# A perceiver layer: attention scores as twelve 32-row products in four row groups instead of four stacked 97-row ones

## The reference, cut to what matters

```python
q = (einsum('bqe,fe->bqf', layernorm(x), wq) + bq).reshape(1, 512, 16, 32)
k = (einsum('bke,fe->bkf', k_full, wk) + bk)      # k_full, v_full: the context twice over
scores = einsum('bqhd,bkhd->bhqk', q, k) / sqrt(32)
attn = softmax(scores, axis=-1)
ctx = einsum('bhqk,bkhd->bqhd', attn, v)
x = x + einsum('bqe,fe->bqf', ctx, out_proj_weight) + out_proj_bias
```

## Time and profile before

| | us |
|---|---|
| median of 3 runs | 1511.66 |
| lowest, highest | 1506.25, 1512.45 |
| span of the profiled execution | 1510.6 |
| PE busy (share of the span) | 1444.6 (96%) |
| DVE busy | 966.9 (64%) |
| ACT busy | 811.0 (54%) |
| 1024 score products (L612): busy | 311.5 |
| 2048 output products (L625): busy | 273.0 |

### The profile page before, as it was taken

The page is one execution under the profiler, slowest core; times in us unless marked ns, Lnnn a source line. Parts: engine busy times, 40 slices in busy tenths (PEclk is TensorE's granted clock), DMA queues, the critical chain, the costliest instruction groups (busy, mean ns, idle before and its releaser), DMA issues. The chain is left out here.

```text
span 1510.6 us, 21218 instructions
## 1 busy us (share of the span) xinstructions
PE 1444.6 (96%) x7952; PEld 910.1 (60%) x7952; DVE 966.9 (64%) x846; ACT 811.0 (54%) x865; POOL 25.9 (2%) x24
## 2 busy tenths in 40 slices
PE   6999999999799999999999999977799999999996
PEld 4888888888433333333333333325688878887884
DVE  7444444443588888888888888865355556555653
ACT  4122122121488888888888888832264445444551
POOL 2000000000300000000000000000000000000000
PEclk9999999999899999999999999998599999999999
DMA  6855455454685555555555555203044544454441
GB/s 199 253 174 207 176 187 201 167 201 161 189 213 115 112 111 111 111 115 118 116 117 116 112 111 111 56 5 110 28 140 156 178 166 164 153 183 163 163 147 57
DMA packets 136180, 214.26 MB, mean 142 GB/s; under 512 B 7624, under 2 KB 40520, under 8 KB 136144
## 3 DMA queue, kind: packets, MB, share of 16 engines
q1 hardware_dynamic: 136144, 213.78, 48.9%
HBM read 159.23 MB, written 51.38 MB: 139 GB/s over the span
## 5 line engine op out<-in xcount | busy, mean ns | idle before, releaser
L659 ACT ACTIVATE at_p<-at_s 128x1024 f32<-128x1024 f32 x512 | 496.8, 1023 | 91.2 <-PE at_s L612 91.0
L679 DVE TENSOR_TENSOR p_sum<-p_sum,at_p 128x2048 f32 (+1 forms) x208 | 476.8, 2292 | 58.4 <-ACT at_p L659 50.9
L612 PEld LDWEIGHTS at_s<-q_stack,at_k 97*128 97x128 f32 x1024 | 172.8, 189 | 249.0 <-ACT at_p L659 162.2
L612 PE MATMUL at_s<-q_stack,at_k 97*128 (+1 forms) x1024 | 311.5, 424 | 7.7 <-PEq L440 7.0
L625 PE MATMUL at_o<-at_p,at_v 128*32 128x512 f32 x2048 | 273.0, 605 | 0.1
L409 ACT ACTIVATE sc_k_hi<-sc_kp,sc_bk 128x512 fp32r<-128x512 f32 x64 | 44.2, 691 | 125.8 <-PE sc_kp L377 125.8
L139 ACT ACTIVATE sc_c_hi<-sc_c 128x2048 fp32r<-128x2048 f32 x16 | 30.7, 1918 | 150.6 <-PE sc_vp L384 137.6
L1267 DVE TENSOR_TENSOR ex_wi_lo<-ei_wi,ex_wi_hi 128x2048 fp32r<-128x2048 f32 x32 | 73.3, 2289 | 51.2 <-ACT ex_wi_hi L1226 51.2
L341 DVE SCALAR_TENSOR_TENSOR sc_k_lo<-sc_kp,sc_bk,sc_k_hi 128x512 fp32r<-128x512 f32 x64 | 48.0, 750 | 89.3 <-ACT sc_k_hi L409 89.2
L349 DVE TENSOR_TENSOR sc_v<-sc_vp,sc_bv 128x512 f32<-128x512 f32 x64 | 44.1, 690 | 88.8 <-PE sc_vp L384 88.8
L1244 ACT ACTIVATE ex_h<-ex_hp,ex_b_cur 128x256 f32<-128x256 f32 x128 | 53.7, 471 | 86.7 <-PE ex_hp L1125 86.2
(11 more groups left out here) (202 smaller groups left out, 1657.6 us busy)
## 6 DMA issues: line engine op xcount, KB each, us to landing
at_k<-k_hi_scratch SPq DMA_DIRECT2D x128, 256.0 KB, 4.7
ei_wi<-w_in SPq DMA_DIRECT2D x32, 1024.0 KB, 7.3
ei_wo<-w_out SPq DMA_DIRECT2D x32, 1024.0 KB, 5.3
sc_c<-ctx_t SPq DMA_DIRECT2D x16, 1024.0 KB, 8.0
k_hi_scratch<-sc_k_hi SPq DMA_DIRECT2D x16, 1024.0 KB, 4.0
k_lo_scratch<-sc_k_lo SPq DMA_DIRECT2D x16, 1024.0 KB, 6.1
at_k<-k_lo_scratch SPq DMA_DIRECT2D x64, 256.0 KB, 4.3
at_v<-v_scratch SPq DMA_DIRECT2D x64, 256.0 KB, 5.0
```

Source lines behind the costliest of these rows:

```text
L612: last = nc.tensor.matmul(s[r][:, a * NQ:(a + 1) * NQ], k[c][:, j, t * P:(t + 1) * P], q_stack[:, bass.ds(it // PER_GROUP * (HG * NQ) + j ...
L659: nc.scalar.activation(p[t % PR][:, pair * 2 * NQ:(pair + 1) * 2 * NQ], s[u % SR][:, :], ACT.Exp, scale=SCALE).then_inc(p_ready[t % PR], 1)
L679: nc.vector.tensor_tensor(sums, sums, p[t % PR][:, :], ALU.add).then_inc(p_summed[t % PR], 1)
```

## The change

The scores of a tile are no longer four products of 97 rows but twelve of 32 rows: for each of hi·hi, lo·hi, hi·lo, one for each head j, on partitions 32j to 32j+31 of keys and queries, accumulated in PSUM. The four heads of a part are on different row groups and write to different banks. Keys are loaded as they lie in scratch, [128, 512] hi and lo, three DMAs a chunk instead of four; there is no row of ones. This form has no shift row, so it is right only while scores are bounded. Therefore the old `attend` is kept as `attend_any`, in a block whose bodies stand in `If(flag < 1)` and which zeroes the accumulators and does the sum again (with two chunk buffers; `BY_PE = (3, 7)` of eight tiles). `find_maxima` moves from ahead of `attend` to behind it, with `attend_any` after it: `attend` runs always and unguarded, then come two guarded blocks.

PE's order changes too: a step is now all scores of tile t+1, then outputs of tile t-1. It waits for both buffers of the tile before its first product, and the two `s_ready` semaphores come in the last of the three parts. The middle iterations are a loop for each head group, so that `g` is a constant: nine iteration bodies instead of three.

```diff
-def load_keys(sp, a, c, g, chunk, k_hi_dram, k_lo_dram, v_dram):
+def load_chunk(sp, a, c, g, chunk, k_hi_dram, k_lo_dram, v_dram):
     keys, feats = bass.ds(chunk * CH, CH), bass.ds(g * P, P)
-    hi = k_hi_dram[feats, keys].rearrange("(j d) n -> d j n", d=D)
-    lo = k_lo_dram[feats, keys].rearrange("(j d) n -> d j n", d=D)
-    for part, src in enumerate((hi, lo, hi)):
-        sp.dma_start(a.k[c][part * D:(part + 1) * D, :, :].bitcast(F32), src).then_inc(a.loaded[c], 16)
+    sp.dma_start(a.k_hi[c][:, :].bitcast(F32), k_hi_dram[feats, keys]).then_inc(a.loaded[c], 16)
+    sp.dma_start(a.k_lo[c][:, :].bitcast(F32), k_lo_dram[feats, keys]).then_inc(a.loaded[c], 16)
     sp.dma_start(a.v[c][:, :, :], v_dram[keys, feats].rearrange("(t p) f -> p t f", p=P)).then_inc(a.loaded[c], 16)
...
-            def scores(it, u):
-                c, t, pair, r = u // 2 // KT, u // 2 % KT, u % 2, u % SR
-                if t == 0 and pair == 0:
+            def scores(it, g, t):
+                c = t // KT
+                if t % KT == 0:
                     pe.wait_ge(loaded[c], LOADS * (it + 1))
...
-                for a in range(2):
-                    j = 2 * pair + a
-                    last = nc.tensor.matmul(s[r][:, a * NQ:(a + 1) * NQ], k[c][:, j, t * P:(t + 1) * P],
-                                            q_stack[:, bass.ds(it // PER_GROUP * (HG * NQ) + j * NQ, NQ)],
-                                            start=True, stop=True)
-                last.then_inc(s_ready[r], 1)
+                for u in (2 * t, 2 * t + 1):
+                    if u >= SR:
+                        pe.wait_ge(p_ready[(u - SR) // 2 % PR], exped(it, u - SR))
+                    else:
+                        wait_reuse(pe, p_ready[s_last[u % SR] // 2 % PR], exped(it, s_last[u % SR]) - 2 * TPR)
+                for part, (keys, queries) in enumerate(((k_hi, q_hi), (k_lo, q_hi), (k_hi, q_lo))):
+                    for j in range(HG):
+                        rows, r = slice(j * D, (j + 1) * D), (2 * t + j // 2) % SR
+                        last = nc.tensor.matmul(s[r][:, j % 2 * NQ:(j % 2 + 1) * NQ], keys[c][rows, t % KT * P:(t % KT + 1) * P],
+                                                queries[rows, g, :],
+                                                start=(part == 0), stop=(part == 2))
+                        if part == 2 and j % 2 == 1:
+                            last.then_inc(s_ready[r], 1)
...
-            def iteration(it, last):
+            def iteration(it, g, ends_group):
                 for t in range(TILES):
-                    for u in (2 * t + AHEAD, 2 * t + AHEAD + 1):
-                        if u < 2 * TILES:
-                            scores(it, u)
-                        elif not last:
-                            scores(it + 1, u - 2 * TILES)
-                    outputs(it, t)
+                    if t + 1 < TILES:
+                        scores(it, g, t + 1)
+                    elif not ends_group:
+                        scores(it + 1, g, 0)
+                    elif g + 1 < NG:
+                        scores(it + 1, g + 1, 0)
+                    if t > 0:
+                        outputs(it, t - 1)
+                    elif not (isinstance(it, int) and it == 0):
+                        outputs(it - 1, TILES - 1)
...
+            scores(0, 0, 0)
+            for g in range(NG):
+                if g == 0:
+                    iteration(0, 0, False)
+                with pe.Fori(1 if g == 0 else 0, PER_GROUP - 1) as i:
+                    iteration(i + g * PER_GROUP, g, False)
+                iteration((g + 1) * PER_GROUP - 1, g, True)
+            outputs(ITERS - 1, TILES - 1)
...
-            with ExitStack() as s:
-                find_maxima(nc, s, k_hi_dram, k_lo_dram, ident, q_stack, bounded)
...
             with ExitStack() as s:
-                attend(nc, s, k_hi_dram, k_lo_dram, v_dram, q_stack, o_acc, p_sum, total_acc, a, late, late_dram)
+                attend(nc, s, k_hi_dram, k_lo_dram, v_dram, o_acc, p_sum, total_acc, a, late, late_dram)
+            with ExitStack() as s:
+                find_maxima(nc, s, k_hi_dram, k_lo_dram, ident, q_stack, bounded)
+            with ExitStack() as s:
+                attend_any(nc, s, k_hi_dram, k_lo_dram, v_dram, q_stack, bounded, o_acc, p_sum, total_acc)
```

More of the change, by code:

```diff
@@ L298, in pair @@
                         sp.wait_ge(stored[0], STORES)
-                        load_keys(sp, a, 0, 0, 0, k_hi_dram, k_lo_dram, v_dram)
+                        load_chunk(sp, a, 0, 0, 0, k_hi_dram, k_lo_dram, v_dram)
                     if not last:
@@ L324, in _ @@
             sp.wait_ge(stored[1], STORES * PAIRS + 16 * (KT - 1))
-        @block.gpsimd
-        def _(pool):
-            nc.gpsimd.memset(a.k[0][3 * D:QROWS, :, :].bitcast(F32), 1.0).then_inc(a.ones_set, 1)
         @block.vector
@@ L504, in _, with attend @@
                 nc.scalar.activation(minus_row[:, :], s[0][0:H * QT, 0:P], ACT.Copy).then_inc(row_ready, 1)
-def load_keys(sp, a, c, g, chunk, k_hi_dram, k_lo_dram, v_dram):
+def load_chunk(sp, a, c, g, chunk, k_hi_dram, k_lo_dram, v_dram):
     keys, feats = bass.ds(chunk * CH, CH), bass.ds(g * P, P)
-    hi = k_hi_dram[feats, keys].rearrange("(j d) n -> d j n", d=D)
-    lo = k_lo_dram[feats, keys].rearrange("(j d) n -> d j n", d=D)
-    for part, src in enumerate((hi, lo, hi)):
-        sp.dma_start(a.k[c][part * D:(part + 1) * D, :, :].bitcast(F32), src).then_inc(a.loaded[c], 16)
+    sp.dma_start(a.k_hi[c][:, :].bitcast(F32), k_hi_dram[feats, keys]).then_inc(a.loaded[c], 16)
+    sp.dma_start(a.k_lo[c][:, :].bitcast(F32), k_lo_dram[feats, keys]).then_inc(a.loaded[c], 16)
     sp.dma_start(a.v[c][:, :, :], v_dram[keys, feats].rearrange("(t p) f -> p t f", p=P)).then_inc(a.loaded[c], 16)
-def attend(nc, ctx, k_hi_dram, k_lo_dram, v_dram, q_stack, o_acc, p_sum, total_acc, a, late, late_dram):
+def attend(nc, ctx, k_hi_dram, k_lo_dram, v_dram, o_acc, p_sum, total_acc, a, late, late_dram):
     sb = lambda n, s, d=F32: ctx.enter_context(nc.sbuf_tensor(n, s, d))
@@ L529, in attend @@
     SR, PR = 3, 4
-    AHEAD = 3
     TPR = TILES // PR
-    LOADS = 4 * 16
-    a.k += [sb(f"at_k{c}", [QROWS, HG, CH], F32R) for c in range(1, CB)]
+    LOADS = 3 * 16
+    a.k_hi += [sb(f"at_k_hi{c}", [P, CH], F32R) for c in range(1, CB)]
+    a.k_lo += [sb(f"at_k_lo{c}", [P, CH], F32R) for c in range(1, CB)]
     a.v += [sb(f"at_v{c}", [P, KT, P]) for c in range(1, CB)]
     a.loaded += [sem(f"at_loaded{c}") for c in range(1, CB)]
-    k, v, loaded, ones_set = a.k, a.v, a.loaded, a.ones_set
+    k_hi, k_lo, v, loaded, q_hi, q_lo = a.k_hi, a.k_lo, a.v, a.loaded, a.q_hi, a.q_lo
     p = [sb(f"at_p{r}", [P, HG * NQ]) for r in range(PR)]
@@ L542, in attend @@
     ones = sb("at_ones", [P, D])
-    zeroed, first_zeroed = map(sem, ("at_zeroed", "at_first_zeroed"))
+    ones_set, zeroed, first_zeroed = map(sem, ("at_ones_set", "at_zeroed", "at_first_zeroed"))
     s_ready = [sem(f"at_s_ready{r}") for r in range(SR)]
@@ L567, in _ @@
         def _(pool):
[L569 to L572, removed]
             nc.gpsimd.memset(ones[:, :], 1.0).then_inc(ones_set, 1)
-            pool.wait_ge(ones_set, CB + 1)
+            pool.wait_ge(ones_set, 1)
             nc.gpsimd.memset(p_sum[:, HG * NQ:], 0.0).then_inc(zeroed, 1)
@@ L587, in iteration @@
                     if c > 0 or not (isinstance(it, int) and it == 0):
-                        load_keys(sp, a, c, it // PER_GROUP, it % PER_GROUP * CB + c, k_hi_dram, k_lo_dram, v_dram)
+                        load_chunk(sp, a, c, it // PER_GROUP, it % PER_GROUP * CB + c, k_hi_dram, k_lo_dram, v_dram)
                 if isinstance(it, int) and it == 0:
@@ L630, in outputs @@
                     if isinstance(it, int) and it == 0:
-                        pe.wait_ge(ones_set, CB + 1)
+                        pe.wait_ge(ones_set, 1)
                     for j in range(HG):
@@ L635, in outputs @@
                 last.then_inc(p_used[r], 1)
-            def iteration(it, last):
+            def iteration(it, g, ends_group):
                 for t in range(TILES):
-                    for u in (2 * t + AHEAD, 2 * t + AHEAD + 1):
-                        if u < 2 * TILES:
-                            scores(it, u)
-                        elif not last:
-                            scores(it + 1, u - 2 * TILES)
-                    outputs(it, t)
-            for u in range(AHEAD):
-                scores(0, u)
-            rolled(pe, ITERS, iteration)
+                    if t + 1 < TILES:
[16 more added lines that the diff above has]
+            outputs(ITERS - 1, TILES - 1)
         @block.scalar
@@ L692, in _, with load_stacked @@
             rolled(dve, ITERS, iteration)
+def load_stacked(sp, k, v, loaded, c, g, chunk, k_hi_dram, k_lo_dram, v_dram):
+    keys, feats = bass.ds(chunk * CH, CH), bass.ds(g * P, P)
+    hi = k_hi_dram[feats, keys].rearrange("(j d) n -> d j n", d=D)
```

(10 more changed lines are left out.)

153 lines of the change are left out of this document (added).

## The result

The change made the kernel slower: 1531.69 us median (1529.42 to 1533.94, 4 runs) against 1510.47 us (4 runs), ratio 1.0146, 95% interval 1.0123 to 1.0168. The profiled execution took 1531.77 us and its span is 1530.0, 19.4 over the span of before.

A forecast was written before the change was run, and what follows sets the result against it. PE was taken to bound the kernel before, an exp-scores loop its plain tiles after. 1510.6 - 17 (attention) - 1 (start) + 5 (blocks) + 3.4 (totals) = 1501, beside the median 1502; range 1486 to 1595.

The forecast's parts named there:

- the likeliest case: Whole kernel: row groups run side by side, 24 to 8 us saved in attention; 1492 to 1515, chance 0.55.
- the 0.05 us from ACT's end to PE's load: In the loop of a plain tile: PE's weight load starts 0.05 us after ACT's exp ends.
- the 0.32 us of the boundary: On PE, one scores group an iteration takes 1.52 us instead of 1.19, added as 0.32 before and after.
- PE's bound, and the work PE sheds: In attention PE bounds the kernel before; a tile's scores hold PE 0.95 us instead of 1.12, tiles with totals 2.80.
- Row groups and loads side by side: In PE's scores, four row-group products cost one, 0.22 us a round, and their weight loads overlap.
- Rivals 1, 2 and 4: PE scores: exposed loads, +37 us, 0.25; loads one after another, +123, 0.17; row groups not side by side, +475, 0.03.
- Rival 3: Dear starts and waits (8 us saved), guarded jump above 5 us: 1508 to 1514; upper end of the first case's 0.55.
- The new loop: Between ACT's exp and PE's scores: 1.02 + 0.05 + 1.01 = 2.08 us a plain tile, above PE's 1.95.
- The start: At the attention's start, PE idles 2 us instead of 7, which may save slow first tiles: -1 us.
- The blocks: Guarded blocks around the attention: two of 5.1 us behind it, less one of 4.9 ahead, +5 us.
- The slower totals: Behind the attention, 32 total products, 3.64 us at full clock, probably run at 1.2 GHz: +3.4 us.
- Fetching of the longer code: Nine iteration bodies instead of three: put at nothing; up to 48 us if fetched anew at each jump.

The follow-up runs named there:

- e3: Changed kernel with its three score buffers used in turn over the whole attention, not restarted each iteration, PE and ACT written out: 1533.4 us.
- e2: Changed kernel with waits that another wait implies taken off PE's scores and ACT's first exp: 1514.5 us.
- e7: Kernel before with only its score buffers used in turn over the whole attention, PE and ACT written out: 1506.8 us.
- e6: Changed kernel with PE and ACT of the attention written out for all 16 iterations, buffers still restarting each iteration: 1548.7 us.
- e8: Changed kernel with score buffers in turn throughout, PE and ACT written out, implied waits off, and both guarded blocks made one: 1497.0 us.
- e11: Changed kernel with score buffers in turn throughout, PE and ACT written out, implied waits off, plus a fourth scores round, lo x lo: 1563.8 us.

## Why the prediction was wrong

It forecast 1502 and a gain; the kernel lost 21 us. The range held the time, the direction and the likeliest case failed. Two terms of the sum failed: the 0.05 us from ACT's end to PE's load, and the 0.32 us of the boundary, carried over unexplained. By its steps:

- **PE's bound, and the work PE sheds: right.** Scores were put at 0.95 us of PE and took 0.90, tiles with totals at 2.80 and took 2.76.
- **Row groups and loads side by side: right.** Rounds of 0.22 were 0.23, and the loads overlap. Rivals 1, 2 and 4 did not occur. Rival 3 was half right: the waits were dearer than its dear end, but the jump over the large body was not. The 3.07x that the Trainium skill ("TensorE: Matmul & The Clock Gate", Measured speedup vs the span model) has for four row tiles is not what this stream shows: a round of four follows the last after 0.23, as long as one 97-row product, so 4x by that pitch. The overlap of loads that the Trainium skill ("TensorEngine Tiling (Array Packing)", Key Properties) allows is there.
- **The new loop: right in kind, mis-sized by 0.09, the largest miss.** The sum had 0.05 from ACT's end to PE's load, from the earlier trace rows, where PE waits for one semaphore only. The scores wait for two, and where the second is an instruction of its own it lies in the loop: 0.12. On ACT the same raised the time from load to exp from 1.03 to 1.08, and in e3 to as much as 1.12. On average 12 x 16 x 0.09 = 17 us; e2 took just this away and got the 2.08 of the forecast.
- **The boundary: the step that failed outright.** "One scores group an iteration takes 1.52 instead of 1.19, 0.32 more" was carried over as a constant, without asking what it was. Three buffers over 32 units begin anew in each iteration, so the first two units wait for the last two exps, units 30 and 31. Before, unit by unit, that cost 0.32 (e7 takes it away). A whole tile waiting for both costs 0.9: with e6 against e3, 15 us. The sum had 2.08 + 0.32 = 2.40 for this tile and it took 3.08, 0.68 x 16 = 11 us short.
- **The start: wrong by some 6 us.** The forecast had -1. Beyond sixteen periods the attention cost 5 more, 13.9 - 16 x 0.55, and most of it lies ahead of the first addition to `o_acc`, 44.9 into the attention instead of 40.0. The granted clock was 0.62 in 393 to 394 and 0.50 from there to 403 us, although PE had idled for only 1.88; before, it was 0.50 until 403 too, but the attention began 5 us later. At that level the loop makes a tile of 2.85 (scores at 396.06, 398.91), and the second outputs start 10.5 us into the attention instead of 7.1. That is 3.4 of the 5; most plain tiles of the first iteration, which is written out, take 2.23 to 2.27, which accounts for about 1 of the rest. No experiment took this apart.
- **The blocks: right.** -4.9 was -5.0, +10.2 was +10.1; e8 confirms the price of one. The slower totals, +3.4, were +2.3: the clock was 0.50 up to 1013 us and 0.76 in 1013 to 1016. The sum rounded two of 5.1 less 4.9, 5.3, to 5.
- **Fetching of the longer code: right at nothing.** The tile in which this loop jumps back (outputs 734.50 to 736.58) takes 2.08, no more than others.

In an iteration the misses are 1.04 for the waits and 0.68 for the boundary, less 0.12 for the tiles with totals: 1.6, or 26 us in sixteen. With the start's 6 that is 32, the distance from the forecast -18 (-17 and the start's -1) to the measured +13.9 in the attention. The prediction said itself that from 0.04 us more in the loop no gain was left; it was right to, and the chance of faster should have been lower, since nothing in the rows priced two waits. (A small misreading without effect: the load of 8 rows has a median of 184 ns, not 185.)

## What to carry to other kernels

Cutting an engine's work gains nothing if the new order closes a latency loop through another engine; count the loop's signals one by one, and from rows with the same number of waits. Take off a wait that another implies wherever it is in such a loop: here that alone was 17 us of 1531. A count of the semaphore instructions in the trace, tile by tile, shows where such waits stand. A ring of buffers that restarts in each iteration of a length it doesn't divide has a stall at each boundary, and an unexplained slow group in an otherwise regular trace deserves its own explanation before a change that touches what it waits for.

## What the runs showed of the hardware

- Rounds of four fp32r products of 32 rows and 512 columns in four row groups follow one another every 0.23 us, one 97-row product's time, loads of 128 columns included (the second round of a tile comes 0.31 to 0.33 after the first). With a fourth round (e11) the pitch stays.
- A second semaphore wait can become an instruction of its own, 51 ns on TensorE and 38 ns on ScalarE, and then costs about 0.09 us a tile where it is on the path. Written out it stood in nearly every tile (15 and 16 of 16, e6), in the loop in 11 and 5 of 16.
- A guarded block that isn't taken cost 5 us here: 4.9 and 5.2 before, 10.1 for two, 5.1 for one that held both bodies (e8).
